# A slot mixer's tokens normed and turned batch by batch inside the attention ahead of it

## The reference

```python
x = x + jnp.tanh(g_xattn[3]) * _L3_xattn_ref(_layernorm(x), ctx_768, ...)
x = x + jnp.tanh(g_ffn[3]) * _L3_ffn_ref(_layernorm(x), ...)
# _L3_ffn_ref, on the normed tokens x:
slot_mean = jnp.broadcast_to(S.mean(axis=1, keepdims=True), (Bx, Tx, Dx))
ctx = jnp.concatenate([x, slot_mean], axis=-1)
h = jax.nn.gelu(ctx @ w1 + b1, approximate=False)
route_logits = (h @ w2 + b2) / (jnp.abs(tau) + 0.1)
topk_vals, topk_idx = jax.lax.top_k(route_logits, TOP_K)
topk_w = jax.nn.softmax(topk_vals, axis=-1)
alpha = (jax.nn.one_hot(topk_idx, NUM_SLOTS, dtype=x.dtype) * topk_w[..., None]).sum(axis=-2)
slot_input = jnp.einsum('bts,btd->bsd', alpha, x)
...
out = jnp.einsum('bts,bsd->btd', alpha, slot_values)
return out @ wo + bo
```

## Time and profile before

| what | us |
|---|---|
| median of three runs | 1810.4 |
| lowest and highest | 1809.12, 1813.86 |
| the profiled execution | 1815.32 |
| its span | 1813.5 |
| fourth attention, first scores to last bn_stats | 1494.2 to 1656.0 |
| slot mixer, first matmul to the end | 1656.1 to 1813.5 |

### The profile page before, as it was taken

One profiled execution on the slowest core, in us unless ns is written; L12 is line 12 of the kernel. 1 busy time (PEld: TensorE's weight loads), 2 busy tenths in 40 slices (PEclk: granted clock), 3 DMA queues, 4 the chain that ended last, 5 costly groups with the idle time before them and its releaser, 6 DMA issues.

```text
span 1813.5 us, 30878 instructions
## 1 busy us (share of the span) xinstructions
PE 1622.6 (89%) x9150; PEld 1154.0 (64%) x9150; DVE 971.4 (54%) x3169; ACT 627.5 (35%) x1780; POOL 318.5 (18%) x434
## 2 busy tenths in 40 slices
PE   6898889859999899999999899799998997777787
PEld 2555555659999766666666567577776446665555
DVE  4778787532222244444444435555554667774664
ACT  3545455412333233333333233133331004443232
POOL 4555555220000210000000000100000112122000
PEclk8999999869999999999999899899998999998797
DMA  4000005149999510000000000100000001210000
GB/s 108 15 17 20 20 19 151 58 165 330 312 322 323 178 30 14 12 12 6 12 12 6 1 7 18 32 20 24 18 18 7 23 26 45 88 43 1 1 18 19
DMA packets 86297, 115.80 MB, mean 64 GB/s; under 512 B 16610, under 2 KB 77762, under 8 KB 81090
## 3 DMA queue, kind: packets, MB, share of 16 engines
q1 hardware_dynamic: 82722, 110.43, 19.2%
q0 software_dynamic: 2432, 4.34, 0.8%
q10 hardware_dynamic: 1056, 0.01, 0.0%
HBM read 104.51 MB, written 6.95 MB: 61 GB/s over the span
## 4 chain that ended last, share of the span: by engine, by line
PE 71%; issue 10%; DVE 7%; ACT 4%; DMA 3%; POOL 2%; SPq 1%; ACTq 1%; DVEq 0%; POOLq 0%
PE bank L2294 14%; PE bank L2407 8%; PE bank L2590 6%; PE bank L2380 5%; PE bank L2683 5%; PE bank L2353 5%; PE bank L2391 4%; PE bank L2437 4%; PE bank L2604 3%; PE bank L2636 3%; PE bank L2345 3%; PE bank L2652 2%; PE bank L2770 2%; DMA work<-in_F_b1c 2%; DVE work L1547 1%
## 5 line engine op out<-in xcount | busy, mean ns | idle before, releaser
L1053 ACT ACTIVATE work<-bank,work 100x361 f32<-100x361 f32 (+1 forms) x272 | 159.0, 591 | 256.2 <-DVE work L1547 235.4
L2407 PEld LDWEIGHTS bank<-work 128*100 128x100 f32 x1760 | 183.6, 170 | 58.5 <-issue 31.4
L1556 DVE COPY work<-bank 128x300 f32<-128x300 f32 (+1 forms) x272 | 123.1, 489 | 174.8 <-PE bank L2391 174.0
L2407 PE MATMUL bank<-work 128*100 128x64 f32 (+1 forms) x1760 | 187.0, 257 | 14.9 <-DVE work L1556 14.8
L2590 PE MATMUL bank<-work 128*128 128x128 f32 x1216 | 143.0, 275 | 2.7 <-DMA work<-in_F_b1c 2.7
L1547 DVE TENSOR_REDUCE work<-bank 100x1 f32<-100x361 f32 x208 | 101.9, 528 | 77.5 <-PE bank L2380 66.5
L2590 PEld LDWEIGHTS bank<-work 128*128 128x128 f32 x1216 | 140.6, 192 | 4.4 <-ACT work L1185 1.9
L1899 DVE SCALAR_TENSOR_TENSOR work<-bank,work 128x128 f32<-128x128 f32 x160 | 56.1, 351 | 161.3 <-PE bank L2590 147.0
L2380 PE MATMUL bank<-work 64*100 64x361 f32 (+1 forms) x512 | 119.4, 544 | 1.1 <-ACT work L1038 0.6
L811 POOL TENSOR_TENSOR work<-work,neg_half 100x1 f32<-100x1 f32 x96 | 52.8, 550 | 373.0 <-DVE work L1503 372.3
L2294 PE MATMUL bank<-L_WkvT,work 96*128 96x512 f32 x192 | 98.2, 637 | 15.6 <-ACT work L1014 14.7
(11 more groups left out here) (313 smaller groups left out, 2866.8 us busy)
## 6 DMA issues: line engine op xcount, KB each, us to landing
work<-in_F_w SPq DMA_DIRECT2D x58, 1024.0 KB, 5.7
work<-in_ctxT SPq DMA_DIRECT2D x64, 135.4 KB, 2.2
work<-in_ctx SPq DMA_DIRECT2D x32, 192.0 KB, 2.5
work<-in_F_b SPq DMA_DIRECT2D x20, 128.0 KB, 6.5
work<-sorted_x SPq DMA_DIRECT2D x20, 128.0 KB, 2.8
sorted_y<-work SPq DMA_DIRECT2D x20, 128.0 KB, 6.1
work<-in_ctx SPq DMA_DIRECT2D x32, 78.8 KB, 2.4
F_weight<-in_F_w SPq DMA_DIRECT2D x2, 1024.0 KB, 6.5
```

The source lines that it names most:

```text
L1053: nc.scalar.activation(pr[:, 0:NK], S_bank[k][0:T, 0:NK], ACT.Exp, bias=nmax[k][0:T, :], accum_out=rsum[j][0:T, h:h + 1]).then_inc(s.exped ...
L1556: nc.vector.tensor_copy(PT[k][:, 0:CH, :], PT_bank[k][:, 0:CH * T].rearrange("p (c t) -> p c t", c=CH)).then_inc(s.probs_copied.sem, 1)
L2407: ins = nc.tensor.matmul(to, PT[k][:, c, :], values, start=(c == 0), stop=(c == CH - 1))
```

## The change

The fourth attention now prepares the mixer's tokens as the second and third do. `mixture` gets an entry for L = 3, so `residual` ends with `mixture_stats`, `attend` calls `mixture_norm(L, t - 1)` between the residual and `o_scale`, `project` ends with `mixture_turn(L, t - 1)`, and the next residual copies the turned tokens (`mixture_keep`) to SXT. GpSimd has a new function, `mixture_tokens`: the power, and for L = 3 a copy of the normed rows from GN to XS, for which DVE's next norm waits (the semaphore `bo_added` counts these copies too). The last batch's norm, turn and copy are made in the mixer. The mixer loses its aggregates, norms, turns and ACT copies. XS and the weights start at `unused_by_3`, SXT and the buffers of pairs 2 and 3 lie behind the weights, where the fourth attention keeps nothing.

```diff
@@ -233,7 +233,6 @@
         gates = sb("gates", [P, 8])
-        x_st6 = sb("x_st6", [P, B, 6])
         neg_half = sb("neg_half", [P, 32])
@@ -357,6 +355,7 @@
+        mixture = {1: mx1, 2: mx2, 3: mx3}
         area = Area()
@@ -437,7 +436,6 @@
-        Fmv, Frs = area.take(B, 2), area.take(B)
         area.at = attention_end
@@ -454,14 +452,12 @@
         area.at = 0
-        XS = area.take(B, D + 1)
         MEAN = area.take(2, 1)
...
         pairs_at = area.at
-        SXT = area.take(2, NTOK)
         HG = area.take(NTOK)
@@ -491,8 +487,10 @@
-        pair = [pair_buffers(k) for k in range(SLOTS_AT_ONCE)]
-        assert area.at >= unused_by_3 and area.at >= pairs_at + 3 * NTOK
+        pair = [pair_buffers(k) for k in range(2)]
+        assert pairs_at + NTOK <= unused_by_3 and area.at <= unused_by_3
+        area.at = unused_by_3
+        XS = area.take(B, D + 1)
         SI, SIT = area.take(D), area.take(2, P)
@@ -501,6 +499,12 @@
         TAU = area.take(2)
+        late_at = area.at
+        SXT = area.take(2, NTOK)
+        assert area.at <= attention_end + 2 * NTOK
+        area.at = late_at
+        pair += [pair_buffers(k) for k in range(2, SLOTS_AT_ONCE)]
+        assert area.at <= attention_end + 2 * NTOK
         slot_loads = []
@@ -777,6 +781,14 @@
+            def mixture_tokens(L, t):
+
+                mixture_rstd(L, t)
+                if L == 3:
+                    wait_count(pool, mx3.ln_x, 3 * (t + 1))
+                    nc.gpsimd.tensor_copy(XS[0:T, bass.ds(t, 1), 0:D], GN[0:T, :].rearrange("p (o d) -> p o d", o=1)
+                                          ).then_inc(mx3.bo_added, 1)
+
             def rows_back(group):
@@ -869,30 +881,17 @@
                     three_deep(pool, attend, lambda t, j: None)
-                elif L == 3:
-                    with pool.Fori(0, B // 2 - 1) as i:
-                        for j in range(2):
-                            norms(2 * i + j + 2, j)
                 else:
...
                     norms(3, 1)
-                    mixture_rstd(L, 0)
+                    mixture_tokens(L, 0)
                     with pool.Fori(1, B // 2 - 1) as i:
...
                             norms(2 * i + j + 2, j)
-                            mixture_rstd(L, 2 * i + j - 1)
-                    mixture_rstd(L, B - 3)
-                    mixture_rstd(L, B - 2)
+                            mixture_tokens(L, 2 * i + j - 1)
+                    mixture_tokens(L, B - 3)
+                    mixture_tokens(L, B - 2)
                 end(pool)
-
-
-            def rstd_x(s, p, last=True):
-
-                begin(pool, p)
-                pool.wait_ge(s.ln_x, B + 1)
-                nc.gpsimd.tensor_tensor(Frs[0:T, :], Frs[0:T, :], neg_half[0:T, 0:B], ALU.pow).then_inc(s.rstd_x, 1)
-                if last:
-                    end(pool)
@@ -933,10 +932,10 @@
                 s = mx3
-                rstd_x(s, 7, last=False)
+                begin(pool, 7)
+                mixture_tokens(3, B - 1)
                 pool.wait_ge(s.bo_scaled, 1)
-                pool.wait_ge(s.ln_x, 2 * B + 1)
                 for u in range(B // 2):
@@ -1236,14 +1235,8 @@
-                for u in range(B // 2):
-                    act.wait_ge(s.x_turned, u + 1)
-                    nc.scalar.copy(SXT[:, :, 2 * T * u:2 * T * (u + 1)].rearrange("p c (m t) -> p m c t", m=2),
-                                   bank[u % 2][:, 0:4 * T].rearrange("p (m c t) -> p m c t", m=2, c=2)).then_inc(s.x_copied, 1)
-                    if u in (3, 5):
-                        gelu((u - 3) // 2)
-                gelu(2)
-                gelu(3)
+                for g in range(B // 4):
+                    gelu(g)
@@ -1416,12 +1409,14 @@
                 wait_count(dve, s.rstd_x, t + 1)
+                if L == 3:
+                    wait_count(dve, s.bo_added, t)
                 nc.vector.tensor_scalar(GN[0:T, :], X[0:T, bass.ds(t, 1), :].rearrange("p o d -> p (o d)"),
...
-                nc.vector.tensor_copy(GXT[:, :, :].rearrange("p c (b t) -> p c b t", b=B)[:, :, bass.ds(t, 1), :],
+                nc.vector.tensor_copy((SXT if L == 3 else GXT)[:, :, :].rearrange("p c (b t) -> p c b t", b=B)[:, :, bass.ds(t, 1), :],
                                       turned[:, TURN_AT:TURN_AT + 2 * T].rearrange("p (c o t) -> p c o t", c=2, o=1)
@@ -1580,7 +1575,7 @@
                         place_rank(t - 2, q % 2, R_bank)
-                    if L in (1, 2) and not (isinstance(t, int) and t == 0):
+                    if L > 0 and not (isinstance(t, int) and t == 0):
                         mixture_keep(L, t - 1, R_bank)
@@ -1593,13 +1588,12 @@
                     apart(dve)
-                    stats = Rst6[0:T, :] if L < 3 else x_st6[0:T, bass.ds(t, 1), :].rearrange("p o n -> p (o n)")
-                    nc.vector.bn_stats(stats, xt).then_inc(s.x_stats.sem, 1)
+                    nc.vector.bn_stats(Rst6[0:T, :], xt).then_inc(s.x_stats.sem, 1)
                     if routed:
...
                         router_stats(t)
-                    if L in (1, 2):
+                    if L > 0:
                         mixture_stats(L, t)
@@ -1675,6 +1669,8 @@
                                 residual(t - 1, 1 - j)
+                        if started:
+                            mixture_norm(L, t - 1)
                     for p in range(PAIRS[L]):
@@ -2000,12 +1996,7 @@
                 begin(dve, 7)
-                wait_for(dve, at[3].x_stats, B)
-                for t in range(B):
-                    nc.vector.bn_aggr(Fmv[0:T, t, :], x_st6[0:T, t, :]).then_inc(s.ln_x, 1)
-                dve.wait_ge(s.ln_x, B)
-                nc.vector.tensor_scalar(Frs[0:T, :], Fmv[0:T, :, 1], LN_EPS, None, ALU.add).then_inc(s.ln_x, 1)
-
+                mixture_norm(3, B - 1)
                 for k in range(SLOTS_AT_ONCE):
@@ -2028,10 +2019,8 @@
-                dve.wait_ge(s.rstd_x, 1)
-                for t in range(B):
-                    nc.vector.tensor_scalar(XS[0:T, t, 0:D], X[0:T, t, :], Fmv[0:T, t, 0:1], Frs[0:T, t:t + 1],
-                                            ALU.subtract, ALU.mult).then_inc(s.ln_x, 1)
+                dve.wait_ge(s.x_turned, 1)
+                mixture_keep(3, B - 1, bank[0])
                 dve.wait_ge(s.consts, 9)
@@ -2167,7 +2156,7 @@
                     dve.wait_ge(s.out, u + 1)
-                    dve.wait_ge(s.bo_added, u + 1)
+                    dve.wait_ge(s.bo_added, B + u + 1)
                     xt = X[0:T, 2 * u:2 * u + 2, :]
@@ -2718,19 +2707,9 @@
-                def tokens_turn(u):
-
-                    wait_count(pe, s.x_copied, u - 1)
-                    pe.wait_ge(s.ln_x, B + 1 + 2 * u + 2)
-                    for m in range(2):
-                        for c in range(2):
-                            ins = tr(bank[u % 2][:, (2 * m + c) * T:(2 * m + c + 1) * T],
-                                     XS[0:T, 2 * u + m, c * P:(c + 1) * P], ident[0:T, 0:T])
-                    ins.then_inc(s.x_turned, 1)
-
                 def hidden(g):
-                    pe.wait_ge(s.x_copied, 2 * (g + 1))
+                    pe.wait_ge(s.x_copied, 4 * (g + 1))
                     if g >= 2:
@@ -2745,15 +2724,10 @@
-                for u in range(4):
-                    tokens_turn(u)
                 hidden(0)
-                for u in range(4, 6):
-                    tokens_turn(u)
+                mixture_turn(3, B - 1, bank[0]).then_inc(s.x_turned, 1)
                 hidden(1)
                 slot_logits(0)
-                for u in range(6, 8):
-                    tokens_turn(u)
                 hidden(2)
@@ -2773,6 +2747,7 @@
                     pe.wait_ge(s.alpha, 3 * (u + 1))
+                    pe.wait_ge(s.bo_added, 2 * (u + 1))
                     if u >= SLOTS_AT_ONCE:
```

More of the change, by code:

```diff
@@ L351, in flamingo_kernel @@
         mx2 = signals(nc, ctx, "linear", "ln_x rstd_x x_turned x_copied logits route exped out combined moved0 moved1 resid")
-        mixture = {1: mx1, 2: mx2}
         mx3 = signals(nc, ctx, "slots", "w_in consts const_sums bo_scaled bo_added ln_x rstd_x x_turned x_copied hidden gelu logits biased picked "
```

## The result

| | kernel before | changed kernel |
|---|---|---|
| median, us (lowest to highest, runs) | 1809.8 (1806.3 to 1813.9, 6) | 1827.6 (1820.7 to 1834.7, 6) |
| ratio to the kernel before | | 1.0092, 95% interval 1.0063 to 1.0122 |
| profiled execution: time, span | 1815.3, 1813.5 | 1834.7, 1832.9 |
| granted clock, mean | 0.952 | 0.945 |

The change costs 16.7 us (1809.8 x 0.0092; the interval is 11 to 22; the medians are 17.8 apart). 1823.0 was predicted, range 1816 to 1835, slower with 0.89. I take the span apart at five marks: the first maximum of the fourth attention (L1542), its first and thirteenth residual row (L1573, which the prediction calls R), TensorE's first mixer matmul (L2701), the first sums of the mixer (L2754).

The account below looks back on a forecast made before the run. VectorE was taken to bound the fourth attention's batches. Loop +13.2, tail +4.5 and mixer front -5.2 sum to +12.5 us on the 1810.4 median, 1822.9, rounded to 1823.0 us; range 1816 to 1835.

Parts of the forecast that it names:

- VectorE sets the period: Fourth attention: VectorE, in order with two GpSimd round trips a batch, sets the 9.88 us period; its slack is 0.44 us.
- The rival with TensorE as the bound: Fourth attention: VectorE's additions disappear in TensorE's time, only two turns (0.3 us) a batch count; 1811 or 1806 us; chance 0.09.
- The price of a batch: Fourth attention's loop: new VectorE work ahead of the scaling costs 1.1 us a batch, +13.2 us over twelve periods.
- that counts each operation to its end: Fourth attention: summing whole VectorE operations puts the next maximum +1.15 us later; overlap can take 0.15 off, lower bound 1.0.
- The 0.1 for the registers of the new waits: Fourth attention's loop: registers computed for the new waits can add 0.1 us a batch.
- The sign that I named, rows of L1573 10.9 to 11.1 us apart: Fourth attention: residual-row starts this far apart in the loop would show the forecast right; a period below 10.3, wrong.
- The clock: Rival, fourth attention: TensorE's waits drop the granted clock in most batches, +1.5 us in each of 12, 1841 us; chance 0.11.
- The sign that I named against myself: Fourth attention's loop: a granted clock of 0.50 in more than two or three batches would show the forecast wrong.
- Copy and turns: Fourth attention's loop: GpSimd's copy was taken as 0 (contention up to 0.5 us a batch), TensorE's two added turns as free.
- The tail: From batch 14 on TensorE bounds; late turns, added turns, scaling and +eps: 1.5+0.3+1.6+0.6+0.5 = +4.5 us.
- The front: Mixer's start: biased logits 12.7 us behind TensorE's first matmul, not 18.4; gain 5.7, or 4.6 at low clock; taken -5.2 us.
- The range: Whole kernel: 1816 to 1835 us, the upper end from 1.2 a batch, 3 contention, 5 clock falls, front only 3.

Follow-up runs that it names:

- the second profile: The changed kernel run once more, unchanged, for its interval and a second profile: median 1828.4 us, ratio 1.0098 to the kernel before.

## Why the prediction was right, point by point

**VectorE sets the period.** Right, and shown from three sides: leave out the root and its wait, 0.64 a batch less; put the scaling ahead of the norm, 0.43 less (10.42 us); put nearly all of the new work into other waits, 0.9 less. The rival with TensorE as the bound is refuted by the tripled turns and by these three.

**The price of a batch.** 1.1 us was taken, with 1.0 as the lower bound; it is 1.0 (ten periods with a mean of 10.85 in place of 9.85). The failing step is "that counts each operation to its end": the added path is 1.50 us and not 1.58, and the maximum starts 0.09 us before the scaling's end, the overlap that I had kept for the bound alone. The 0.1 for the registers of the new waits did not show. 12 x 1.0 is 12.0, and the two long periods bring 1.6 more: 13.6 (13.8 in the second profile) where 13.2 stood: nearly the right sum, by luck, with two errors in it. The sign that I named, rows of L1573 10.9 to 11.1 us apart, was missed by a little, for the same reason; TensorE's wait for the scaling was 1.1 to 1.25 us where I had 1.3.

**The clock.** I had argued that waits of 0.6 to 0.8 us leave the clock at 1.00; one of those waits was 1.0 us, which would have been a stronger case. The rival's mechanism does occur, with four falls in twelve periods in place of one in most, and at 1.6 us in place of 18. The sign that I named against myself, a clock of 0.50 in more than two or three batches, came true while the forecast held: it was badly chosen, since a fall's price is that of its place. A short one cost nothing in the changed kernel and 1.04 us in the kernel with the scaling ahead. The Trainium skill ("TensorE: Matmul & The Clock Gate", section "HAM oscillation — how this bites in real kernels") describes a loop in which every step starts cold, with matmuls in each step that are shorter than the wait for the next slice. Here TensorE is busy 8.8 us of a period and waits 1.16 us at a time, and most batches ran at 1.00.

**Copy and turns.** Both taken as free, both free: 0 for the copy, 0 for four more turns at the full clock.

**The tail.** 4.5 us; over the first profile of before it measured 4.4 in one profile, and 6.6 in the other, where the clock was low for longer (0.82 against 0.90, and 0.91 before). The step's error is that it counts the late work at one clock. Its five terms were not measured one by one; only their sum is.

**The front.** The terms add to 5.7 and I took 5.2; it gave 5.9 and 6.4 (26.36 - 20.45, 26.36 - 19.91). The first hidden group ran at 1.59 us, the high clock. The biased logits at +12.60 and +12.06 answer to +12.7. The table load did lie behind the first hidden group, and the first logits started at +9.50 (1691.77), where the terms put them at +9.4:

```profile
1691.77 0.92 PE L2724 MATMUL bank<-work 128*100 128x64 f32 x8 [0.56 <-ACT work L1235]
```

But TensorE ran the second hidden group meanwhile, and only 0.56 us of wait was left. So the 1.28 us lies on the path as the prediction has it, while at most 0.56 of it would go with the load.

**The range.** Its upper end was said to add up to +25; the terms that it names give 14.4 + 4.5 + 3 + 5 - 3 = 23.9. The result lies inside either way.

**The sum.** From the first maximum on, the changed kernel's profiles are 10.2 and 14.4 us longer than the first of before, and 12.5 was predicted. The medians say 16.7 and 17.5, with intervals down to 11 and 13. The stages ahead differ by more than this remainder between profiles of one kernel, so it may be chance. The other versions point to a small part that is not: in the twelve rows of the table that are not the kernel before, (ratio - 1) x 1811 is above the profile's own difference from 318.05 us (the mean of the two profiles of before) by 1.9 us on average, from -1.4 to 7.9. That the stages ahead are slower in the changed kernels by some 2 us is not excluded, and stays open.

## What to carry to other kernels

Read where an engine waits before you place new work on it: the same statistics and norm cost 1.0 us a batch between a result and the engine that waits for it, and 0.08 in the engine's own waits for a round trip to GpSimd. Count the slack of the old order once (0.44 us here), then charge the rest in full. And before a GpSimd instruction is moved away from operations that it slows, look at which ones it will meet next.

## What the runs showed of the hardware

An operation of VectorE that works on SBUF alone and meets a GpSimd operation can take as long as that one, whatever its own length: 1.37 and 1.38 us in place of 0.43 for 100x256, about 1.2 each in place of 0.21 for 100x64, beside adds of 1.2 to 1.4. Not every one does: four MAX8 of 100x64 took 0.61 us and a MATCH_REPLACE8 0.21 beside the same adds, as without them. The biased logits, which read PSUM, took 0.69 us beside the adds and without them. I had not expected the alphas to be hit, and had priced contention by the ratio in the earlier trace rows. The Trainium skill ("SBUF — State Buffer", section "SBUF: two separate sides") calls the pair of ports that the two engines share an exclusive lock, held for a whole instruction; the alphas, one per add, agree with that.

The granted clock does not fall only behind a wait as long as the 2.00 us of the earlier trace rows. In each of the four profiles whose periods hold waits of TensorE of up to 1.25 us (the changed kernel twice, rows copied by ScalarE, turns tripled) it fell four times in twelve periods. With that wait filled or the root left out (longest wait 0.69 and 0.68 us) it fell twice, with the scaling ahead of the norm (0.83) once, and before (1.01) and with the work in the waits (0.76) not at all. So the longest wait alone does not say where the clock falls, and what does was not found here. The same instructions at the mixer's start took 7.97 us in one profile and 11.16 in another by the clock alone. A difference of 3 us in one profile's stretch is no evidence without its clock beside it.
